# A gated cross-attention and expert block: how the joined projection is centered, and which engine takes the x statistics

## The reference

```
def _layernorm(x, axis=-1, eps=1e-05):
    m = jnp.mean(x, axis=axis, keepdims=True)
    v = jnp.var(x, axis=axis, keepdims=True)
    return (x - m) / jnp.sqrt(v + eps)

# cross-attention: q = layernorm(x), k = v1 = ctx
_proj = lambda x: (x @ W1.T + b1) @ W2.T + b2        # W1, W2: 256 x 256
qk = einsum('bqd,bkd->bqk', _proj(q), _proj(k)) / 16 + mask
x = x + tanh(g_xattn) * softmax(qk) @ ctx

# experts: s = layernorm(x), 8 experts, each token goes to the one with the largest logit
h = s @ w1[e];  a, g = split(h, 2);  y = (silu(a) * g) @ w2[e]
x = x + tanh(g_ffn) * y * max(softmax(s @ router_w + router_b))
```

## Time and profile before

| | |
|---|---|
| median of three runs | 452.51 us |
| the profiled execution's own time | 450.66 us |
| its span (first to last instruction) | 448.6 us |
| TensorE busy | 399.7 us (89%) |
| GpSimd busy | 246.2 us (55%) |
| VectorE busy | 213.7 us (48%) |
| ScalarE busy | 175.9 us (39%) |
| mean granted TensorE clock | 0.955 |
| first tile of the expert loop | from 99 us |

### The profile page before, as it was taken

One profiled execution on the slowest core, in us unless ns is written; L12 is line 12 of the kernel. 1 busy time (PEld: TensorE's weight loads), 2 busy tenths in 40 slices (PEclk: granted clock), 3 DMA queues, 4 the chain that ended last, 5 costly groups with the idle time before them and its releaser, 6 DMA issues.

```text
span 448.6 us, 9824 instructions
## 1 busy us (share of the span) xinstructions
PE 399.7 (89%) x2431; PEld 346.0 (77%) x2432; DVE 213.7 (48%) x520; ACT 175.9 (39%) x337; POOL 246.2 (55%) x323
## 2 busy tenths in 40 slices
PE   5998872149999999999999999999999999999990
PEld 4887751037888888888888888888888888888880
DVE  4888995842443443344443444433434434444340
ACT  1276650014543454545532344445433543233230
POOL 2566989020875677887773258728852676232221
PEclk9999996558999999999999999999999999999997
DMA  7951222652333044433342103433331011001010
GB/s 212 361 188 51 97 99 80 102 200 84 119 118 117 23 147 173 145 117 117 123 161 80 36 18 117 135 112 124 117 117 36 4 36 36 24 24 28 24 35 11
DMA packets 29850, 44.27 MB, mean 99 GB/s; under 512 B 8377, under 2 KB 25581, under 8 KB 27791
## 3 DMA queue, kind: packets, MB, share of 16 engines
q1 hardware_dynamic: 24095, 34.58, 23.4%
q0 software_dynamic: 3456, 9.24, 6.3%
q10 hardware_dynamic: 2288, 0.33, 0.5%
HBM read 35.57 MB, written 8.96 MB: 99 GB/s over the span
## 4 chain that ended last, share of the span: by engine, by line
PE 79%; POOL 8%; DVE 6%; DMA 2%; issue 2%; ACT 1%; DVEq 0%; SPq 0%; POOLq 0%; ACTq 0%
PE py L1093 22%; PE pa L1075 22%; PE pg L1075 21%; PE ph L1085 7%; POOL w_lo L411 2%; PE px L1060 2%; POOL rstd L395 2%; PE ps_s L1004 1%; DMA ctx_in<-in_ctx 1%; POOL slot_iota L432 1%; PE ps_p L948 1%; DMA x_sorted<-residual_rows,idx_gather 1%; DVE x_all L728 1%; PE ps_xt L920 1%; POOL mask_c L387 1%
## 5 line engine op out<-in xcount | busy, mean ns | idle before, releaser
L875 DVE TENSOR_TENSOR ht_lo<-ph,ht_hi 128x512 fp32r<-128x512 f32 x70 | 48.4, 692 | 135.9 <-ACT ht_hi L610 135.9
L481 POOL TENSOR_TENSOR w_lo<-staging,w_hi x84 | 107.4, 1307 | 6.7 <-ACT w_hi L631 4.0
L610 ACT CAST ht_hi<-ph 128x512 fp32r<-128x512 f32 x70 | 41.1, 587 | 121.3 <-PE ph L1085 86.0
L1093 PE MATMUL py<-w_hi,ht_hi 128*128 x280 | 81.3, 290 | 0.8 <-DVE out_tile L883 0.8
L1093 PE MATMUL py<-w_hi,ht_lo 128*128 x280 | 78.4, 280 | 0.0
L1093 PE MATMUL py<-w_lo,ht_hi 128*128 x280 | 78.3, 280 | 0.0
L470 POOL DMA_INDIRECT out<-out_tile,idx_now x34 | 34.7, 1019 | 72.0 <-DVE out_tile L883 71.3
L1075 PE MATMUL pa<-w_hi,xt_hi 128*128 (+1 forms) x140 | 58.8, 420 | 0.8 <-ACT xt_hi L592 0.8
L439 POOL DMA_INDIRECT x_sorted<-residual_rows,idx_now x34 | 35.6, 1048 | 40.8 <-DVE x_norm L858 22.7
L1075 PE MATMUL pg<-w_hi,xt_hi 128*128 (+1 forms) x140 | 56.1, 401 | 0.0
L1075 PE MATMUL pa<-w_lo,xt_hi 128*128 (+1 forms) x140 | 56.1, 401 | 0.0
(11 more groups left out here) (167 smaller groups left out, 577.5 us busy)
## 6 DMA issues: line engine op xcount, KB each, us to landing
staging<-in_L_ffn_w SPq DMA_DIRECT2D x24, 1024.0 KB, 4.9
residual_rows<-x_all SPq DMA_DIRECT2D x8, 532.0 KB, 3.6
x_all<-in_x SPq DMA_DIRECT2D x8, 512.0 KB, 9.9
x_sorted<-residual_rows,idx_now POOLq DMA_INDIRECT x34, 3.9
out<-out_tile,idx_now POOLq DMA_INDIRECT x34, 2.5
w_in<-in_L_xattn_W SPq DMA_DIRECT2D x2, 256.0 KB, 4.7
ctx_in<-in_ctx SPq DMA_DIRECT2D x1, 308.0 KB
mask_in<-in_fside_1xSxS ACTq DMA_DIRECT2D x1, 308.0 KB, 11.2
```

Source lines behind the costliest of these rows:

```text
L481: lo = nc.gpsimd.tensor_tensor(out=w_lo[:, bass.ds(dst + q * QW, QW)], in0=staging[:, bass.ds(src + q * QW, QW)], in1=w_hi[:, bass.ds(dst ...
L610: nc.scalar.copy(ht_hi[:, j], ph[j][:]).then_inc(hhi_ready[j], 1)
L875: nc.vector.tensor_tensor(out=ht_lo[:, j], in0=ph[j][:], in1=ht_hi[:, j].bitcast(FP32), op=ALU.subtract).then_inc(hlo_ready[j], 1)
L1093: last = mm(py[:, 0:D], ht[:, j, c * P:(c + 1) * P], w[:, bass.ds(slot + (DC * PW + (j * HC + c) * D), D)], start=j == 0 and n == 0, stop= ...
```

## The change

The centered matrix is no longer a second product of a centered W1. TensorE transposes `m_t` into the PSUM bank `ps_o[1]`, ahead of the keys' projection, and VectorE takes the mean there and subtracts it on the way to `m_c` (`m_mean`, three passes). ScalarE now scales the values, both halves of the keys and the bias. Group 1's statistics go to ScalarE: a Copy pass with a summing output per batch, a small multiply to minus the mean, a Square pass with that as bias and a summing output per batch; GpSimd's `norm1` of group 1 divides by 256 and adds eps. The passes' unneeded full output goes to the part of `staging` where the third weight piece will land, so that piece's transfer waits for `square_ready`. Six groups (`EARLY = 6`) now have their statistics before round 0, and GpSimd does their `norm1` in the order 0, 2, 3, then both first masks, then 1, 4, 5.

```diff
+        m_mean = sb0("m_mean", [P, 2, DC])
+        x_seen = staging[:, DC * PW:DC * PW + B * D].rearrange("p (b d) -> p b d", b=B)
+        x_sum = sb0("x_sum", [P, 2, B])
+        x_square = sb0("x_square", [P, B])
...
-        EARLY = 5
+        EARLY = 6
+        X_ORDER = (0, 2, 3, 1, 4, 5, 6, 7)
...
+                if k == DC:
+                    sp.wait_ge(square_ready, 1)
...
             def norm1(first_group, end_group):
-                pool.wait_ge(mv1_ready, end_group)
-                link(nc.gpsimd.tensor_scalar(var_eps1[:, at], mv1[:, at, :, 1], EPS, None, ALU.add))
+                if first_group == 1:
+                    pool.wait_ge(square_ready, 1)
+                    link(nc.gpsimd.tensor_scalar(var_eps1[:, 1], x_square[:], 1.0 / D, EPS, ALU.mult, ALU.add))
+                else:
+                    pool.wait_ge(mv1_ready, end_group if end_group == 1 else end_group - 1)
+                    link(nc.gpsimd.tensor_scalar(var_eps1[:, at], mv1[:, at, :, 1], EPS, None, ALU.add))
...
-            for g in range(EARLY - 1):
+            for g in X_ORDER[:3]:
                 norm1(g, g + 1)
             mask1(0)
             mask1(1)
-            norm1(EARLY - 1, EARLY)
+            for g in X_ORDER[3:EARLY]:
+                norm1(g, g + 1)
...
+            nc.scalar.activation(values[:, :, 0:D], ctx_in[:], ACT.Copy, scale=tanh_g[0:KEYS, 0:1]).then_inc(values_ready, 1)
             act.wait_ge(m_psum, 1)
             nc.scalar.copy(m_t[:], ps_p[:].rearrange("p (c d) -> p c d", c=DC)).then_inc(mt_ready, 1)
+
+            act.wait_ge(x_loaded[1], 16)
+            for b in range(B):
+                last = nc.scalar.activation(x_seen[:, b], x_all[:, 1, b, 0:D], ACT.Copy, accum_out=x_sum[:, 0, b:b + 1])
+            last.then_inc(x_sum_step, 1)
...
-            act.wait_ge(keys_psum, 1)
-            nc.scalar.mul(keys_t[:, 0, :, 0:KEYS], ps_p[:, 0:KB].rearrange("p (b k) -> p b k", b=B), SCALE
-                          ).then_inc(keys_ready, 1)
+            for dc in range(DC):
+                act.wait_ge(keys_psum, dc + 1)
+                nc.scalar.mul(keys_t[:, dc, :, 0:KEYS],
+                              (ps_p, ps_o[1])[dc][:, 0:KB].rearrange("p (b k) -> p b k", b=B), SCALE).then_inc(keys_ready, 1)
+            act.wait_ge(bias_psum, 1)
+            nc.scalar.mul(bias_c[:], ps_s[1][:, 0:KB], SCALE).then_inc(bias_ready, 1)
+
+            act.wait_ge(x_sum_step, 1)
+            nc.scalar.mul(x_sum[:, 1], x_sum[:, 0], -1.0 / D).then_inc(x_sum_step, 1)
+            act.wait_ge(x_sum_step, 2)
+            for b in range(B):
+                last = nc.scalar.activation(x_seen[:, b], x_all[:, 1, b, 0:D], ACT.Square, bias=x_sum[:, 1, b:b + 1],
+                                            accum_out=x_square[:, b:b + 1])
+            last.then_inc(square_ready, 1)
...
-            nc.vector.tensor_reduce(w1_mean[:, 0], w1_in[:], AX.X, ALU.add).then_inc(w1c_step, 1)
-            nc.vector.tensor_scalar(w1_mean[:, 1], w1_mean[:, 0], 1.0 / D, None, ALU.mult).then_inc(w1c_step, 1)
-            nc.vector.tensor_tensor(out=w1_c[:], in0=w1_in[:], in1=w1_mean[:, 1].unsqueeze(2).to_broadcast([P, DC, D]),
-                                    op=ALU.subtract).then_inc(w1c_step, 1)
...
+            dve.wait_ge(mc_psum, 1)
+            m_wide = ps_o[1][:].rearrange("p (c d) -> p c d", c=DC)
+            nc.vector.tensor_reduce(m_mean[:, 0], m_wide, AX.X, ALU.add).then_inc(mean_step, 1)
+            nc.vector.tensor_scalar(m_mean[:, 1], m_mean[:, 0], 1.0 / D, None, ALU.mult).then_inc(mean_step, 1)
+            nc.vector.tensor_tensor(out=m_c[:], in0=m_wide, in1=m_mean[:, 1].unsqueeze(2).to_broadcast([P, DC, D]),
+                                    op=ALU.subtract).then_inc(mc_ready, 1)
...
+            pe.wait_ge(mt_ready, 1)
+            for oc in range(DC):
+                for dc in range(DC):
+                    last = nc.tensor.transpose(ps_o[1][:, oc * D + dc * P:oc * D + (dc + 1) * P],
+                                               m_t[:, dc, oc * P:(oc + 1) * P], ident[:])
+            last.then_inc(mc_psum, 1)
             for k in range(DC):
                 pe.wait_ge(ctxt_ready[k], 1)
-            pe.wait_ge(mt_ready, 1)
...
-            pe.wait_ge(w1c_step, 3)
-            for oc in range(DC):
-                for k in range(DC):
-                    last = mm(ps_o[1][:, oc * D:(oc + 1) * D], w2_t[:, k, oc * P:(oc + 1) * P], w1_c[:, k], start=k == 0,
-                              stop=k == DC - 1)
-            last.then_inc(mc_psum, 1)
```

More of the change, by code:

```diff
@@ L134, in flamingo_block @@
         ctx_in = sb0("ctx_in", [KEYS, B, D])
-        w1_in, w2_in, w1_c, w2_t = (sb0(name, [P, DC, D]) for name in ("w1_in", "w2_in", "w1_c", "w2_t"))
-        w1_mean = sb0("w1_mean", [P, 2, DC])
+        w1_in, w2_in, w2_t = (sb0(name, [P, DC, D]) for name in ("w1_in", "w2_in", "w2_t"))
+        m_mean = sb0("m_mean", [P, 2, DC])
+        x_seen = staging[:, DC * PW:DC * PW + B * D].rearrange("p (b d) -> p b d", b=B)
+        x_sum = sb0("x_sum", [P, 2, B])
+        x_square = sb0("x_square", [P, B])
         ctx_t = sb0("ctx_t", [P, DC, KB])
@@ L223, in flamingo_block @@
         router_c_ready = sem("router_c_ready")
-        w1c_step = sem("w1c_step")
+        mean_step = sem("mean_step")
+        x_sum_step = sem("x_sum_step")
         m_psum = sem("m_psum")
@@ L237, in flamingo_block @@
         vr_ready = sem("vr_ready")
+        square_ready = sem("square_ready")
         bn1_ready = sem("bn1_ready")
@@ L523, in _ @@
             nc.scalar.activation(tanh_g[:], gates_in[:], ACT.Tanh).then_inc(tanh_ready, 1)
+            act.wait_ge(ctx_loaded, 16)
+            act.wait_ge(tanh_ready, 1)
+            nc.scalar.activation(values[:, :, 0:D], ctx_in[:], ACT.Copy, scale=tanh_g[0:KEYS, 0:1]).then_inc(values_ready, 1)
             act.wait_ge(m_psum, 1)
             nc.scalar.copy(m_t[:], ps_p[:].rearrange("p (c d) -> p c d", c=DC)).then_inc(mt_ready, 1)
+            act.wait_ge(x_loaded[1], 16)
+            for b in range(B):
+                last = nc.scalar.activation(x_seen[:, b], x_all[:, 1, b, 0:D], ACT.Copy, accum_out=x_sum[:, 0, b:b + 1])
+            last.then_inc(x_sum_step, 1)
             def copy_xt(g):
@@ L643, in stats1 @@
             def stats1(g):
+                n = g + 1 if g < 1 else g
                 dve.wait_ge(x_loaded[g], 16)
@@ L647, in stats1 @@
                 last.then_inc(bn1_ready, 1)
-                dve.wait_ge(bn1_ready, g + 1)
+                dve.wait_ge(bn1_ready, n)
                 for b in range(B):
@@ L671, in _ @@
             stats1(0)
-            stats1(1)
             dve.wait_ge(bq_psum, 1)
@@ L676, in _ @@
             nc.vector.tensor_copy(bq_wide[:], bq[:].unsqueeze(2).to_broadcast([P, DC, P])).then_inc(bq_step, 1)
-            stats1(2)
+            dve.wait_ge(mc_psum, 1)
+            m_wide = ps_o[1][:].rearrange("p (c d) -> p c d", c=DC)
+            nc.vector.tensor_reduce(m_mean[:, 0], m_wide, AX.X, ALU.add).then_inc(mean_step, 1)
+            dve.wait_ge(mean_step, 1)
+            nc.vector.tensor_scalar(m_mean[:, 1], m_mean[:, 0], 1.0 / D, None, ALU.mult).then_inc(mean_step, 1)
+            dve.wait_ge(mean_step, 2)
+            nc.vector.tensor_tensor(out=m_c[:], in0=m_wide, in1=m_mean[:, 1].unsqueeze(2).to_broadcast([P, DC, D]),
+                                    op=ALU.subtract).then_inc(mc_ready, 1)
             dve.wait_ge(kp_psum, 1)
             nc.vector.tensor_scalar(kp_t[:, 1], ps_s[0][:, 0:KB], bq[:, 1:2], None, ALU.add).then_inc(kp_ready[1], 1)
[L680 to L685, removed]
-            stats1(3)
[L687 to L691, removed]
+            stats1(2)
+            stats1(3)
             stats1(4)
+            stats1(5)
             def router_values():
@@ L705, in mask_and_max @@
                     dve.wait_ge(probs_ready, g - 1)
-                dve.wait_ge(rstd1_ready, g + 1)
+                dve.wait_ge(rstd1_ready, X_ORDER.index(g) + 1)
                 for b in range(B):
@@ L981, in _ @@
                               stop=k == DC - 1)
-            last.then_inc(keys_psum, 1)
+                last.then_inc(keys_psum, 1)
             pe.wait_ge(bq_step, 2)
```

3 lines of the change are left out of this document (removed).

## The result

The changed kernel took 460.73 us (median of 6 runs, 459.98 to 462.87), the kernel before 452.04 beside it (6 runs, 450.87 to 454.33): ratio 1.0186, 95% interval 1.0153 to 1.0219. The profiled execution took 462.87 us, its span is 461.1 (448.6 before), its mean granted clock 0.956.

What follows compares the result with a forecast made beforehand. Bound: GpSimd's rounds from group 0's second norm, before an expert loop moving as a whole. Preparation 1.0, VectorE's block 1.7 and GpSimd's pair 1.3 give 4.1 us earlier: 446.6 profiled, 448.4 median; range 446.4 to 450.6.

Steps and rivals of the forecast that it cites:

- Everything after shifts by 4.1: After GpSimd's second norm of group 0, all later work comes 4.1 us earlier; profiled execution 446.6 us.
- D: Rival, preparation and rounds: transposes replacing products let TensorE's clock fall; 8.5 us slower, time 461; chance 0.03.
- D's own sign: The deciding test for the slower rival: TensorE's clock reads below 1.00 anywhere between 13 and 35 us.
- 8.2 + 4.4: Charges at the 1.2 GHz level: 8.2 us for the preparation's products, 4.4 us for one round.
- the four transposes: TensorE, ahead of the keys' projection: 0.44 us replaces products of 1.73, net 1.29 us less.
- Rival B: Preparation and first tile: gain above 4.5 us, from an earlier clock rise or less GpSimd waiting; 446.0 to 448.0; chance 0.08.
- The mean in PSUM: VectorE, preparation: ready at 15.1 to 15.8 while TensorE asks at 16.66, so it costs nothing.
- Copy passes: ScalarE, group 1's sums: four passes at 0.50 us each, floor 0.345, ceiling 0.80, from 12.9 to 14.9.
- The bias scaling: Preparation, moved from VectorE (0.48 us) to ScalarE: estimated 0.54 us by the pointer-operand price; the moved scalings cost nothing.
- four statistics blocks: VectorE, groups 2 to 5 in a row at 1.71 us each, so first masked scores start at 23.2.
- second norm of group 0: GpSimd, start of the rounds: 35.8 instead of 39.88, 4.1 us earlier; it sets the time of all that follows.
- rival A: Preparation's passes eat more: gain 2.9 to 3.2 us, 2.5 with GpSimd late too; 449.3 to 450.0; chance 0.17.

Runs made afterwards that it cites:

- the second profile: The changed kernel run and profiled once more, unaltered; 459.58 us.
- e7: Changed kernel with x_norm on ScalarE and GpSimd writing 1/sigma straight into the row; 448.95 us, 0.988 of the kernel before.
- e8: Kernel before with x_norm on ScalarE and GpSimd writing 1/sigma straight into the row; 451.73 us, 0.9972 of the kernel before.
- e1: Changed kernel with 13 one-column memsets at the head of VectorE's program; 449.8 us, 0.9889 of the kernel before.
- e3: Changed kernel with each w_lo piece in eight GpSimd slices instead of four; 450.8 us, 0.9917 of the kernel before.
- e4: Changed kernel with x_norm on ScalarE and one more small GpSimd instruction per second norm for the sign; 449.54 us, 0.9889 of the kernel before.
- f2: Changed kernel with 5 memsets at the head of VectorE's program; 450.41 us, one run.
- e2: Kernel before with 3 one-column memsets at the head of VectorE's program; 452.95 us, 0.9987 of the kernel before.
- e5: Kernel before with 19 memsets at the head of VectorE's program; 454.07 us, one run.
- e6: Kernel before with 51 memsets at the head of VectorE's program; 453.48 us, one run.
- f1: Kernel before with 128 memsets at the head of VectorE's program; 451.21 us, one run.
- d1: Changed kernel with group 1's statistics back on VectorE (five groups early, old order) and 5 memsets; 452.02 us, 0.9965 of the kernel before.
- d2: Kernel before with only the move of group 1's statistics to ScalarE, plus 8 memsets; 451.61 us, 0.9947 of the kernel before.
- d3: Kernel before with only the move of group 1's statistics to ScalarE, without memsets; 451.34 us, one run.
- e9: Kernel before with 115 memsets at the head of VectorE's program; 467.98 us, one run.
- e10: Kernel before with 243 memsets at the head of VectorE's program; 466.96 us, one run.

## Why the prediction was wrong

**The step that failed** is this one: "What follows is the expert loop, which the change does not touch. It can only move as a whole." So the sum ends with "Everything after shifts by 4.1", and the loop's own change stands in it at nothing. It was read from the diff and from TensorE's idle time there, next to none. The loop did not move as a whole: it grew by 13.6 us, because its `x_norm` passes stood 0.18 us ahead of a boundary of GpSimd's slices and now stand 0.10 ahead. No rival had it. D named 461 us, and 460.73 was measured, but that is luck: D's cause was a fall of the clock under the transposes. In the second profile the clock stood at the full level from 12.1 to 59.9 us, over the transposes and most rounds, and the time was 459.58 all the same. The first profile did run at the half level until 17.6, which D's own sign would have taken for its case; it was a late rise, not a fall, and cost 2.5 us and not the 12.6 (8.2 + 4.4) that D charges.

**Point by point**, from the second profile, where the clock rose as early as before:

- TensorE: keys' projection at 13.49 (forecast 13.6); the four transposes took 0.53 (0.44), and `bq` ahead of them ended 0.2 sooner than before. In the first profile they ran at the half level; that a rise at 12.4 could come at 17.6 was no term of the sum (about 2.5 us). Rival B had the clock as a gain only.
- The mean in PSUM: its last pass ended at 15.15, ahead of the need. Nothing lost, as forecast.
- ScalarE's passes, in the first profile:

```profile
12.93 0.42 ACT L545 ACTIVATE staging<-x_all 128x256 f32<-128x256 f32 x1
13.25 0.19 ACT L545 ACTIVATION_READ_ACCUMULATOR staging<-x_all 128x1 f32 x1
13.34 0.41 ACT L545 ACTIVATE staging<-x_all 128x256 f32<-128x256 f32 x1
...
22.97 0.51 ACT L571 ACTIVATE staging<-x_all,x_sum 128x256 f32<-128x256 f32 x1
...
23.48 0.49 ACT L571 ACTIVATE staging<-x_all,x_sum 128x256 f32<-128x256 f32 x1
```

  Copy passes stand 0.40 to 0.41 apart (forecast 0.50), squares 0.49 to 0.51 (0.50); the accumulator read overlaps the end of its own pass and the start of the next. The bias scaling took 0.43 on ScalarE (L565 at 22.42), less than VectorE's 0.48 and than the 0.54 that the prediction estimates beside it (at a price for pointer operands; the scale here is a constant).
- VectorE: four statistics blocks at 1.71, first masked scores at 22.90 (23.2). The x^T copy of group 2 at 26.74 on the chain (27.1), the added attention at 31.66 (32.1).
- GpSimd: second norm of group 0 at 35.40 (35.8), released by VectorE's statistics of the new x; it had waited 1.68, so rival A's late GpSimd did not come. Routing at 74.96 (75.3).
- The sum of these: 4.43 us earlier at the routing against 4.1 forecast, and 4.2 us by e7 and e8. That half was right in mechanism, and in size where the clock rises early; in the first profile, with the late rise, it came to 1.65. The loop outweighed it three to one. Together they give the medians: 13.1 longer in the loop (343.93), first tile 4.2 sooner (94.31), is 8.9, and the medians differ by 8.7.

**What stays open.** Why the jump, and the step behind it, are slow at some places, and why 0.16 us and not less is enough at a boundary. Whether the change makes the late rise of the clock likelier: it rose between 16.9 and 17.6 in five of seven profiles that keep the whole change (the changed kernel twice, e1, e3, e4, e7, f2), and between 10.9 and 12.8 in nine that lack it or half of it (before, e2, e5, e6, e8, f1, d1, d2, d3); but at 17.0 in e9 and 20.6 in e10 too, which have nothing of the change. In five profiles (e5, e6, e9, e10, d1) it also fell to the half level for 3.4 to 6.8 us between 39 and 52 us; its cost is not worked out here.

## What to carry to other kernels

Code that a diff does not touch still moves: instructions added or taken ahead of a loop shift its place in the engine's program, and the time of its jump with it. Before calling a tight loop fixed, look how near its short passes on VectorE stand to the start of a long GpSimd instruction; a distance under 0.2 us can be lost by such a shift. Smaller slices make a miss cheap (0.85 us at the most in e3), and the pass on ScalarE never missed. When an untouched loop slows, put a few useless instructions at the head of the engine's program before blaming the change. Try two numbers of them: a padding can also land the loop on a slow place, as in e9.

## What the runs showed of the hardware

- VectorE's jump back to the head of its loop takes 0.197 us at six places tried and 0.27 to 0.31 at three others (medians of the loop's passes; the first two or three are longer). The sequencer's step behind it takes 0.10 at the six and 0.20 to 0.22 at the three.
- Between two GpSimd instructions in a row, a VectorE pass of 0.40 us gets in if it starts 0.16 us or more ahead of the second (28 of the 29 such passes in the two profiles); at 0.04 to 0.11 all thirteen waited for the second to end. That is 0.95 us of a tile lost for 0.08 us of lateness. Near the limit both happen: in the second profile of the changed kernel one at 0.12 got in and one at 0.15 did not.
- TensorE's granted clock rises from the 1.2 to the 2.4 GHz level at 12.1 us in one execution of a kernel and at 17.6 in another. The routing came 2.8 us later in the second, 2.5 of it from products at the half level.
